# A graph network on one core: Elu and normalization by tile inside the projection of an attention layer, turned tiles copied by ScalarE, row terms stored beside the maximum

## The chip, the core and the metric

The kernel runs on one core of one Trainium2 chip. The metric is the device time of one execution in microseconds, from runs of the compiled program; the profile is of one execution more. All times below are microseconds (us) unless marked ns. PE is TensorE (matmul; PEld is its weight load), DVE VectorE, ACT ScalarE, POOL GpSimd, SP SyncE, which here only issues transfers.

## The reference

2500 nodes of 256 features and 40000 edges go through four parts: two graph attention layers of 8 heads of 32, a product with a masked matrix, three graph convolutions with a dense decoder, and one more attention of 4 heads of 64. Between the parts stand residual sums and a normalization with ReLU. The three attention layers are what the change touches.

```
def gat_conv(x, W, al, ar, b, src, dst):          # layers 1 and 2, H = 8, D = 32
    h = (x @ W).reshape(N, H, D)
    el = jnp.einsum('nhd,hd->nh', h, al)
    er = jnp.einsum('nhd,hd->nh', h, ar)
    e = jax.nn.leaky_relu(el[src] + er[dst], NEG_SLOPE)
    m = jax.ops.segment_max(e, dst, num_segments=N)
    ex = jnp.exp(e - m[dst])
    s = jax.ops.segment_sum(ex, dst, num_segments=N)
    alpha = ex / s[dst]
    out = jax.ops.segment_sum(alpha[:, :, None] * h[src], dst, num_segments=N)
    out = out.reshape(N, H * D) + b
    return jax.nn.elu(out)
...
x = gat_conv(features, W0, al0, ar0, b0, src, dst)
x = gat_conv(x, W1, al1, ar1, b1, src, dst)
```

Layer 1 reads relu(layernorm(x)); layer 2 reads the Elu of layer 1; the last attention (`_gat_head`, the same shape with 4 heads) reads relu(layernorm) of the decoder's output.

## The kernel before, in words

The 2500 nodes are 20 tiles (NT) of 128 rows. A matrix C of edge counts (16-bit, 20 x 2560 columns) stays in the core's memory, so that an attention is dense work on 128 x 1280 or 128 x 640 pieces of it. The program is a row of phases. Each phase has one instruction stream for each engine, and all engines meet at its end: the semaphores that the phase used are cleared, then comes a barrier (`Phase.__exit__`, which does so only where the phase owned a semaphore).

`attention(gat, nh, dh, split, norm, sgn, AB, scatter)` is called three times and has three phases:

1. The projection (lines 653 to 769). With `norm`, DVE takes mean and variance of all 20 tiles (L618, L624), ACT the root (L635), DVE the reciprocal and the shift (L627, L630). DVE multiplies the weights by the attention vectors and sums (the products, L696 and L700; they need the transfers of L679 and L681, or of L672 and L676 in the last attention). Then comes a loop over the tiles: ACT writes the tile `xn` (L738 with the normalization and ReLU, L741 a plain copy), PE turns it in two transposes (L753, "turn"), DVE copies it out of PSUM as `xT` (L710), PE multiplies by the weights (L760, "product", four instructions), and DVE takes the result: attention terms `AB` (L714), features `HB` (L715) and the largest magnitude `hmax` (L717). PSUM has two buffers of each kind. DVE's order in a step is xT of tile t, then the result of tile t-1. After the last tile PE turns the row terms (L769), DVE scales them (L726), SP stores them to DRAM (L685) and waits until they have landed.
2. The maximum and the exponentials (lines 787 to 930): a maximum over all nodes, four Exp by ACT, then ten rounds that write the factors UV and VP.
3. The heads (lines 945 to 1157): for each head and each part of C, SP loads one broadcast row of terms (`rows`, L991, two buffers), ACT compares (L1015), DVE masks (L1059, L1062), PE multiplies (L1146, L1154).

Between layer 1 and layer 2 stands a phase of its own, `elu` (L1165): five batches of four tiles, each with DVE bias sums (L1215), a minimum (L1220), ACT's Exp (L1256), a maximum (L1235) and a sum (L1241). Its result in HB is what L741 copies.

Of the kernel before, what the change touches and what calls it, by code (L numbers as in the profile page):

```python
# [15 lines left out]
P = 128  # L16
N = 2500
E = 40000
D = 256
# [48 lines left out]
def build(nc, x, src, dst, ew, gat0, gat1, sage, dec, gat3, out):  # L68
# [4 lines left out]
    with top:  # L73
# [567 lines left out]
        def attention(gat, nh, dh, split, norm, sgn, AB, scatter):  # L641
# [9 lines left out]
            HV = HB[:, :].rearrange("p (t c) -> p t c", t=NT)[:, :, 0:nh * (dh + 1)].rearrange("p t (h c) -> p t h c", c=dh + 1)  # L651

            with Phase() as ph:
# [3 lines left out]
                xn = ph.sb("xn", [P, 2, D], f32)  # L657
                xT = ph.sb("xT", [P, 2, D], f32)
                blocks = [(b, min(P, RT - b)) for b in range(0, RT, P)]
                rT = ph.sb("rT", [P, len(blocks) * P], f32)  # L660
                m_ = norm_memory(ph) if norm else None
                psT = [ph.ps(f"psT{u}", [P, D]) for u in range(2)]
                psH = [ph.ps(f"psH{u}", [P, W2]) for u in range(2)]
                psR = ph.ps("psR", [P, len(blocks) * P])
                s_tR, s_rT, s_w, s_wx, s_xn, s_T, s_xT, s_M, s_out, s_v, s_rd = (
                    ph.sem(n) for n in ("tR", "rT", "w", "wx", "xn", "T", "xT", "M", "out", "v", "rd"))
                block = ph.enter_context(nc.Block())
                @block.sync
                def _(sp):
                    if split:  # L670
# [12 lines left out]
                    sp.wait_ge(s_rT, len(blocks))  # L683
                    for n, (b, w) in enumerate(blocks):
                        sp.dma_start(rowd[b:b + w, :], rT[0:w, n * P:(n + 1) * P]).then_inc(s_rd, 16)  # L685
                    sp.wait_ge(s_rd, 16 * len(blocks))

                @block.vector
                def _(v):
                    ch = Chain(v, s_v)  # L690
                    if norm:
                        norm_vector(v, m_)
                    v.wait_ge(s_w, 16 * (3 * nh if split else 3))
                    for k in range(K):
                        for j in range(2):
                            ch(v.tensor_tensor(prod[:, 2 * k + j, :], Wx[:, k, 0:D], av[:, j, :], ALU.mult))  # L696
                    ch.wait()
                    for k in range(K):
                        for j in range(2):
                            last = v.tensor_reduce(Wx[:, k, D + j * nh:D + (j + 1) * nh],  # L700
                                                   prod[:, 2 * k + j, :].rearrange("p (h d) -> p h d", d=dh), AX.X,
                                                   ALU.add)
                    last.then_inc(s_wx, 1)
                    v.sem_inc(s_out, 6)
                    v.sem_inc(s_xT, 2)

                    def turned(t, u):
                        hold(v, s_T, t + 3)
                        hold(v, s_M, t + 1)
                        v.tensor_copy(xT[:, u, :], psT[u][:, :]).then_inc(s_xT, 1)  # L710

                    def result(t, u):
                        hold(v, s_M, t + 3)
                        v.tensor_copy(ABv[:, ds(t, 1), :], psH[u][:, D:W2].unsqueeze(1)).then_inc(s_out, 1)  # L714
                        v.tensor_copy(HV[:, ds(t, 1), :, 0:dh].rearrange("p t h c -> p (t h) c"),  # L715
                                      psH[u][:, 0:D].rearrange("p (h c) -> p h c", c=dh)).then_inc(s_out, 1)
                        v.tensor_reduce(hmax[:, ds(t, 1)], psH[u][:, 0:D], AX.X, ALU.max,  # L717
                                        apply_absolute_value=True).then_inc(s_out, 1)

                    def step(t, before, u):  # L720
                        turned(t, u)
                        result(before, 1 - u)
                    skewed(v, turned, step, result)
                    for n, (b, w) in enumerate(blocks):
                        v.wait_ge(s_tR, len(blocks))
                        v.tensor_scalar(rT[0:w, n * P:(n + 1) * P], psR[0:w, n * P:(n + 1) * P], BIG, None, ALU.mult  # L726
                                        ).then_inc(s_rT, 1)

                @block.scalar
                def _(a):  # L730
                    if norm:
                        norm_scalar(a, m_)
                    with a.Fori(0, NT // 2) as i:
                        for u in range(2):
                            t = i * 2 + u
                            hold(a, s_T, t + 1)
                            if norm:
                                a.activation(xn[:, u, :], XB[:, ds(t * D, D)], ACT.Relu, bias=m_["nmr"][:, ds(t, 1)],  # L738
                                             scale=m_["sd"][:, ds(t, 1)]).then_inc(s_xn, 1)
                            else:  # L740
                                a.activation(xn[:, u, :], HB[:, ds(t * TW, D)], ACT.Copy).then_inc(s_xn, 1)  # L741

                @block.tensor
                def _(pe):
                    pe.sem_inc(s_T, 2)
                    pe.sem_inc(s_M, 2)
                    pe.wait_ge(s_wx, 1)

                    def turn(t, u):
                        hold(pe, s_xn, t + 1)  # L750
                        hold(pe, s_xT, t + 1)
                        for k in range(K):
                            m = pe.transpose(psT[u][:, k * P:(k + 1) * P], xn[:, u, k * P:(k + 1) * P], ident[:, :])  # L753
                        m.then_inc(s_T, 1)

                    def product(t, u):
                        hold(pe, s_xT, t + 3)
                        hold(pe, s_out, t * 3 + 3)
                        for k in range(K):
                            m = pe.matmul(psH[u][:, :], xT[:, u, k * P:(k + 1) * P], Wx[:, k, :], start=k == 0, stop=k == K - 1)  # L760
                        m.then_inc(s_M, 1)

                    def step(t, before, u):
                        turn(t, u)
                        product(before, 1 - u)
                    skewed(pe, turn, step, product)
                    pe.wait_ge(s_out, 3 * NT + 6)
                    for n, (b, w) in enumerate(blocks):
                        pe.transpose(psR[0:w, n * P:(n + 1) * P], AB[:, RT + b:RT + b + w], ident[:, :]).then_inc(s_tR, 1)  # L769
# [6 lines left out]
            TH = NT * nh  # L776
            heads = Phase()
            with heads as hp:
                cB = hp.sb("cB", [P, TH], f32)
# [165 lines left out]
                with Phase() as ph:  # L945
# [39 lines left out]
                    def _(sp):  # L985
                        with sp.Fori(0, nh) as h:
                            for p in range(PARTS):
                                if TWO:
                                    hold(sp, s_Mn, (h * PARTS + p + 1) * len(TWO))
# [1005 lines left out]
```

## Time and profile before

| what | value |
|---|---|
| median of 3 runs | 2344.32 us (2344.3 to 2346.5) |
| the profiled execution's own time | 2345.53 us |
| its span | 2343.7 us |
| granted TensorE clock, mean | 0.909 |
| PE busy | 1751.7 us (75%) |
| DVE busy | 1668.3 us (71%) |
| ACT busy | 1378.9 us (59%) |
| POOL busy | 300.0 us (13%) |

The busy shares are means over phases with different limits. The change is read from the phases it touches: the first projection begins at 342.9 and its second phase at 393.0; the Elu phase begins at 779.9, the second projection at 804.4 and its second phase at 851.2; the last projection begins at 1936.5 and its second phase at 1985.7. The granted clock is a share of 2.4 GHz: 0.50 is 1.2 GHz, 1.00 is 2.4 GHz.

### The profile page before, as it was taken

The page shows a single profiled execution, that of the slowest core. Times are in us where ns is not written, and L with a number is a line of the kernel's source. Part 1 is how long each engine was busy: PE and PEld are TensorE (multiplying, and loading weights), DVE is VectorE, ACT ScalarE, POOL GpSimd, SP SyncE. Part 2 cuts the span into 40 slices and gives each one's busy share as a digit, 9 for nine tenths or more (in the row PEclk, how much of TensorE's full clock was granted, in tenths as well). Part 3 has the DMA queues.
Part 4 walks back from the last instruction along what each step waited for, and adds up shares of the span by engine and source line. Part 5 has one row for each costly group of instructions (what it writes and reads, how often), then busy time and mean ns, then how long its engine had stood idle before and what let it go on. Part 6 is the DMA issues. An engine that isn't in the chain of part 4 may idle for free. (4 is left out here: it accounts for less than half of the span.)

```text
span 2343.7 us, 65803 instructions
## 1 busy us (share of the span) xinstructions
PE 1751.7 (75%) x21987; PEld 1349.0 (58%) x21987; DVE 1668.3 (71%) x3799; ACT 1378.9 (59%) x2202; POOL 300.0 (13%) x460
## 2 busy tenths in 40 slices
PE   3998865599888336889981399994977995388881
PEld 1333323588888226888881256662546983388881
DVE  6988877899999678999997511113333246799997
ACT  0245763899999238999992411212122352699993
POOL 2465401556100020000000000000000000200000
PEclk9999987799999678999995699997998997699996
DMA  1000000111010001010001110000001010000002
GB/s 60 1 2 2 3 11 2 35 36 34 27 36 25 12 2 40 32 36 36 36 13 51 45 39 0 0 0 6 1 0 37 23 55 10 18 19 25 19 19 89
DMA packets 29718, 54.87 MB, mean 23 GB/s; under 512 B 10222, under 2 KB 20820, under 8 KB 29104
## 3 DMA queue, kind: packets, MB, share of 16 engines
q1 hardware_dynamic: 24608, 43.89, 5.5%
q0 software_dynamic: 4880, 7.80, 1.0%
q8 instruction: 158, 2.59, 0.4%
q14 instruction: 72, 0.59, 0.1%
HBM read 43.19 MB, written 8.49 MB: 22 GB/s over the span
## 5 line engine op out<-in xcount | busy, mean ns | idle before, releaser
L1146 PE MATMUL ps<-R,M 128*128 128x132 f16 (+1 forms) x8640 | 809.4, 221 | 217.4 <-DVE M L1059 112.2
L1015 ACT ACTIVATE Rm<-rows,cB 128x1280 bf16<-128x1280 f32 (+1 forms) x832 | 885.0, 1156 | 35.3 <-DMA rows<-rowd 16.1
L1146 PEld LDWEIGHTS ps<-R,M 128*128 128x128 f16 x8640 | 728.8, 97 | 260.7 <-issue 127.8
L1154 PE MATMUL ps<-HB,C 128*128 128x66 f16 x6400 | 597.0, 193 | 0.0
L1059 DVE TENSOR_TENSOR M<-Rm,C 128x1280 f16<-128x1280 bf16 (+1 forms) x832 | 555.4, 691 | 55.6 <-ACT Rm L1015 48.9
L1154 PEld LDWEIGHTS ps<-HB,C 128*128 128x128 f16 x6400 | 572.4, 97 | 0.0
L1419 PE MATMUL psA<-R,C 128*128 128x512 f16 (+1 forms) x1200 | 253.6, 350 | 96.5 <-POOL ones L1471 41.1
L546 DVE TENSOR_SCALAR ohc<-cells,near 128x1280 f16<-128x1280 f16 x387 | 214.0, 553 | 53.2 <-PE acc L571 47.4
L571 PE MATMUL acc<-ohc,ohl 128*128 128x420 f16 (+1 forms) x1161 | 244.5, 349 | 2.0 <-issue 0.4
L1419 PEld LDWEIGHTS psA<-R,C 128*128 (+1 forms) x1200 | 119.2, 99 | 193.7 <-issue 109.1
L1062 DVE SCALAR_TENSOR_TENSOR M<-rows,cN,C 128x1280 f16<-128x1280 f32 x128 | 197.9, 1546 | 0.0
L571 PEld LDWEIGHTS acc<-ohc,ohl 128*128 128x128 f16 x1161 | 90.2, 98 | 148.9 <-DVE ohl L548 86.7
L420 POOL DMA_INDIRECT wd<-wv,wi x104 | 122.7, 1180 | 135.1 <-issue 76.9
L530 ACT ACTIVATE C<-acc 128x420 f16<-128x420 f32 (+1 forms) x120 | 55.7, 543 | 125.6 <-PE acc L571 125.6
L1581 DVE TENSOR_SCALAR rdeg<-psD 128x1 f32 (+1 forms) x20 | 3.2, 158 | 171.6 <-ACT tl L1551 171.6
L548 DVE TENSOR_SCALAR ohl<-lows,bT 128x128 f16<-128x128 f16 x387 | 102.0, 264 | 0.0
L1049 DVE TENSOR_TENSOR Mn<-C,M 128x640 f16<-128x640 f16 x192 | 93.5, 487 | 0.6
L1149 PE MATMUL ps<-VS,C 128*128 128x130 f16 x640 | 88.3, 221 | 0.0
L1146 PE MATMUL ps<-R,Mn 128*128 128x130 f16 x960 | 86.8, 220 | 0.0
L760 PE MATMUL psH<-Wx,xT 128*128 128x272 f32 (+1 forms) x240 | 72.1, 426 | 16.0 <-DVE AB L714 14.3
L753 PE MATMUL psT<-ident,xn 128*128 128x128 f32 x120 | 24.9, 296 | 71.3 <-DVE Wx L700 71.3
L1510 PE MATMUL ps<-xT,W 128*128 128x128 f32 x640 | 76.3, 278 | 1.0 <-ACT xT L1555 1.0
(280 smaller groups left out, 2276.8 us busy)
## 6 DMA issues: line engine op xcount, KB each, us to landing
rows<-rowd SPq DMA_DIRECT2D x32, 640.0 KB, 3.8
rows<-rowd SPq DMA_DIRECT2D x16, 320.0 KB, 3.4
xd<-R SPq DMA_DIRECT2D x1, 2560.0 KB, 8.4
xr<-xd SPq DMA_DIRECT2D x20, 128.0 KB, 2.0
xd<-HB SPq DMA_DIRECT2D x1, 2560.0 KB, 9.9
xr<-xd POOLq DMA_DIRECT2D x1, 2560.0 KB, 9.3
R<-in_x SPq DMA_DIRECT2D x1, 2432.0 KB
R<-in_x POOLq DMA_DIRECT2D x1, 2432.0 KB
```

The costliest lines, as they stand in the source:

```text
L420: g.indirect_dma_start(out=wd[:, :], out_offset=bass.IndirectOffsetOnAxis(ap=m["wi"][w][:, :], axis=0), in_=m["wv"][w][:, :], in_offset=No ...
L546: v.tensor_scalar(ohc[:, u, :], cells[:, :], near[:, q % 2, ds(k, 1)], None, ALU.is_equal).then_inc(s_oh, 1)
L548: v.tensor_scalar(ohl[:, u, :], lows[:, :], bT[:, ds(k, 1)], None, ALU.is_equal).then_inc(s_oh, 1)
L571: ins = pe.matmul(bank(b, q % 2), ohl[:, u, :], ohc[:, u, d0 * NT:d1 * NT], start=first_, stop=True, skip_group_check=True)
L1015: a.activation(Rm[:, s % SG, :], rows[:, p % 2, :], ACT.Relu, bias=cB[:, ds(h + s * nh, 1)]).then_inc(s_R, 1)
L1049: v.tensor_tensor(Mn[:, u, :], Cs, M[:, u, :], ALU.subtract).then_inc(s_Mn, 1)
L1059: v.tensor_tensor(M[:, u, :], Rm[:, u, :], Cs, ALU.min).then_inc(s_M if s in ONE else s_cut, 1)
L1062: v.scalar_tensor_tensor(M[:, u, :], rows[:, p % 2, :], cN[:, ds(h + s * nh, 1)], Cs, ALU.is_gt, ALU.mult).then_inc(s_M, 1)
L1146: m = pe.matmul(region(p % 2, r), lhsT, rhs, start=first, stop=True, skip_group_check=True)
L1149: m = pe.matmul(region(p % 2, r), C[:, s * NP + p * W + (r % TP) * P:][:, 0:P], VS[:, TURNED.index(s), :, ds(h * cw, cw)], start=False, st ...
L1154: m = pe.matmul(both[:, :, cw:2 * cw], C[:, s * NP + p * W + r * P:][:, 0:P], VP[:, s, :, ds(h * cw, cw)], start=False, stop=True, skip_gr ...
L1419: m = pe.matmul(psA[:, :], lhsT, SPv[:, s, :, :].rearrange("p l c -> p (l c)"), start=s == 0, stop=s == NT - 1)
```

## The change

- The Elu phase between layers 1 and 2 is gone. Layer 2's projection loads the bias and does the Elu tile by tile: DVE adds the bias (`biased`), ACT writes relu(-z) and then exp of its negative (`negative`, `power`), DVE writes max(e - 1, z) (`unit`), and PE turns that.
- With normalization the statistics go in batches of five tiles (`stats`, `roots`, `scales`). The products come behind the first batch, the later batches stand between results.
- `xT` is copied by ACT (`turned`), no longer by DVE. The loops are written out.
- The turning and storing of the row terms is in the second phase, with ACT's copy in place of DVE's; the first two loads of `rows` are issued there too, and the third phase issues only the others. The two semaphores of `rows` now belong to the phase `heads` that encloses the second and third.

The core of the diff:

```diff
 @block.vector
+    def unit(t):
+        v.wait_ge(s_e, t + 1)
+        if t >= 4:
+            v.wait_ge(s_T, t - 3)
+        v.scalar_tensor_tensor(y[:, t % 4, :], e[:, t % 4, :], -1.0, z[:, t % 4, :], ALU.add,
+                               ALU.max).then_inc(s_y, 1)
...
     if norm:
-        norm_vector(v, m_)
...
+        stats(0)
+        products()
+        stats(1)
+        scales(0)
+        for b in range(NT // FIVE):
+            if b + 2 < NT // FIVE:
+                stats(b + 2)
+            if b + 1 < NT // FIVE:
+                scales(b + 1)
+            for t in batch(b):
+                result(t)
+    else:
+        for i in range(NT + 4):
+            if i < NT:
+                biased(i)
+            if i == 3:
+                products()
+            if 0 <= i - 2 < NT:
+                unit(i - 2)
+            if i >= 4:
+                result(i - 4)
 @block.scalar
+    def turned(t):
+        a.wait_ge(s_T, t + 1)
+        if t >= 2:
+            a.wait_ge(s_M, t - 1)
+        a.activation(xT[:, t % 2, :], psT[t % 2][:, :], ACT.Copy).then_inc(s_xT, 1)
+    if norm:
+        roots(0)
+        for i in range(NT + 1):
+            if i < NT:
+                normal(i)
+                if i % FIVE == 2 and i // FIVE + 1 < NT // FIVE:
+                    roots(i // FIVE + 1)
+            if i:
+                turned(i - 1)
+    else:
+        for i in range(NT + 3):
+            if i < NT:
+                negative(i)
+            if 0 <= i - 1 < NT:
+                power(i - 1)
+            if i >= 3:
+                turned(i - 3)
 @block.tensor
+    def turn(t):
+        pe.wait_ge(s_y, t + 1)
+        if t >= 2:
+            pe.wait_ge(s_xT, t - 1)
...
+    def product(t):
+        pe.wait_ge(s_xT, t + 1)
+        if t == 0:
+            pe.wait_ge(s_wx, 2 * K)
+        if t >= 2:
+            pe.wait_ge(s_out, (t - 1) * 3)
...
+    for i in range(NT + 1):
+        if i < NT:
+            turn(i)
+        if i:
+            product(i - 1)
 # second phase
+    @block.sync
+    def _(sp):
+        for n, (b, w) in enumerate(blocks):
+            sp.wait_ge(s_rT, n + 1)
+            sp.dma_start(rowd[b:b + w, :], rT[0:w, n * P:(n + 1) * P]).then_inc(s_rd, 16)
+        sp.wait_ge(s_rd, 16 * len(blocks))
+        for q in range(2):
+            sp.dma_start(rows[:, q, :], row_terms[q, 0:1, :].to_broadcast([P, W])).then_inc(s_row[q], 16)
...
-attention(gat0[0:3], 8, 32, False, True, 1, AB, True)
-elu(R[:, :], HB, gat0[3], 8, False, pitch=TW)
-attention(gat1[0:3], 8, 32, False, False, 1, AB, False)
+attention(gat0[0:3], 8, 32, False, None, 1, AB, True)
+attention(gat1[0:3], 8, 32, False, gat0[3], 1, AB, False)
```

How it moves DVE's work at the head of the first projection (st and mv are the statistics, sd and nmr the scale and the shift, prod and Wx the products). Before:

```order
L618 BN_STATS st<-R 128x6 x20
L624 BN_AGGR mv<-st 128x2 x20
L627 RECIPROCAL sd<-sd 128x20
L630 SCALAR_TENSOR_TENSOR nmr<-mv,sd 128x20
L696 TENSOR_TENSOR prod<-Wx,av 128x256 x4
L700 TENSOR_REDUCE Wx<-prod 128x8 x4
L710 COPY xT<-psT_83 128x256
```

DVE at the same place now:

```order
L710 BN_STATS st<-R 128x6 x5
L713 BN_AGGR mv<-st 128x2 x5
L700 TENSOR_TENSOR prod<-Wx,av 128x256 x4
L704 TENSOR_REDUCE Wx<-prod 128x8 x4
L710 BN_STATS st<-R 128x6 x5
L713 BN_AGGR mv<-st 128x2 x5
L718 RECIPROCAL sd<-sd 128x5
L721 SCALAR_TENSOR_TENSOR nmr<-mv,sd 128x5
L710 BN_STATS st<-R 128x6 x5
L713 BN_AGGR mv<-st 128x2 x5
L718 RECIPROCAL sd<-sd 128x5
L721 SCALAR_TENSOR_TENSOR nmr<-mv,sd 128x5
```

The products moved ahead of the first scales, and only then come the first reciprocal and shift that release ACT's first tile.

DVE at the head of the second projection (AB and HB are the result's terms and features), before:

```order
L696 TENSOR_TENSOR prod<-Wx,av 128x256 x4
L700 TENSOR_REDUCE Wx<-prod 128x8 x4
L710 COPY xT<-psT_179 128x256
L597 UNCONDITIONAL_BRANCH
L597 ISA
L149 REGISTER_ALU
L710 COPY xT<-psT_180 128x256
L149 REGISTER_ALU
L714 ISA
L714 COPY AB<-psH_181 128x16
L715 ISA
L715 COPY HB<-psH_181 128x8x32
```

DVE at the same place now, where z is the sum with the bias, e ACT's exponential and y the Elu's result:

```order
L727 TENSOR_TENSOR z<-R,bias 128x256 x3
L734 SCALAR_TENSOR_TENSOR y<-e,z 128x256
L727 TENSOR_TENSOR z<-R,bias 128x256
L696 TENSOR_TENSOR prod<-Wx,av 128x256 x4
L704 TENSOR_REDUCE Wx<-prod 128x8 x4
L734 SCALAR_TENSOR_TENSOR y<-e,z 128x256
L727 TENSOR_TENSOR z<-R,bias 128x256
L734 SCALAR_TENSOR_TENSOR y<-e,z 128x256
L740 COPY AB<-psH_178 128x16
L741 COPY HB<-psH_178 128x8x32
L742 TENSOR_REDUCE hmax<-psH_178 128x1
```

The copy of xT left DVE; in a step stand now z of tile i, y of tile i-2 and the result of tile i-4, and the products come behind the fourth z.

SP around the second layer's row terms, before:

```order
L679 DMA Wx<-in_L_gnn_W 128x2x256
L681 DMA av<-in_L_gnn_al 128x256
L681 DMA av<-in_L_gnn_ar 128x256
L685 DMA rowd<-rT 128x128
L685 DMA rowd<-rT 32x128
L98 UNCONDITIONAL_BRANCH
L984 UNCONDITIONAL_BRANCH
L986 UNCONDITIONAL_BRANCH
L986 ISA
L991 ISA
L991 DMA rows<-rowd 128x1280
```

SP at the same place now:

```order
L678 DMA bias<-in_L_gnn_b 128x256
L688 DMA Wx<-in_L_gnn_W 128x2x256
L690 DMA av<-in_L_gnn_al 128x256
L690 DMA av<-in_L_gnn_ar 128x256
L98 UNCONDITIONAL_BRANCH
L911 UNCONDITIONAL_BRANCH
L915 DMA rowd<-rT 128x128
L915 DMA rowd<-rT 32x128
L918 DMA rows<-rowd 128x1280 x2
L98 UNCONDITIONAL_BRANCH
L1078 UNCONDITIONAL_BRANCH
L1085 DMA rows<-rowd 128x1280 x14
```

The stores and the first two loads moved past the end of the projection (its L98), the loads past the end of the second phase as well; the bias comes ahead of the weights.

## Rows read from the trace of the kernel before

**Rows 1.** Windows: stretch, length, busy of PE, PEld, DVE, ACT, POOL, clock, DMA, GB/s.
```profile
358.60:389.20 30.60, 25.09 (x114) 18.26 (x112) 23.16 (x78) 9.62 (x16) 0.00 (x0) 0.97 0.00 0
816.00:847.30 31.30, 25.26 (x114) 18.30 (x112) 23.24 (x78) 6.68 (x16) 0.00 (x0) 0.98 0.00 0
```

**Rows 2.** Timeline, first projection's head: start, duration, engine, line, [idle before <-releaser].
```profile
342.90 6.63 DVE L618 BATCH_NORM_STATS2 st<-R 128x6 f32<-128x256 f32 x20 [7.34 <-PEq L101]
...
349.57 1.43 DVE L624 BATCH_NORM_AGGREGATE mv<-st 128x2 f32<-128x6 f32 x20
...
352.29 1.09 ACT L738 ACTIVATE xn<-R,nmr,sd 128x256 f32 x2 [0.94 <-DVE nmr L630]
...
356.68 2.15 PE L760 MATMUL psH<-Wx,xT 128*128 128x272 f32 x4 [0.58 <-DVE xT L710]
...
359.06 0.19 DVE L714 COPY AB<-psH 128x16 f32 x1 [2.21 <-PE psH L760]
```

**Rows 3.** Timeline, PE in the first projection's loop: turn, product, next turn.
```profile
363.55 0.38 PE L753 MATMUL psT<-ident,xn 128*128 128x128 f32 x2
...
363.83 1.16 PE L760 MATMUL psH<-Wx,xT 128*128 128x272 f32 x4
...
364.82 0.38 PE L753 MATMUL psT<-ident,xn 128*128 128x128 f32 x2
```

**Rows 4.** Timeline, the first projection's last tile, its row terms, the next phase.
```profile
386.29 0.41 DVE L710 COPY xT<-psT 128x256 f32<-128x256 f32 x1
...
386.97 0.76 PEld L760 LDWEIGHTS psH<-Wx,xT 128*128 128x128 f32 x4 [1.01 <-issue]
387.00 1.16 PE L760 MATMUL psH<-Wx,xT 128*128 128x272 f32 x4 [0.61 <-DVE AB L714]
...
388.30 0.19 DVE L714 COPY AB<-psH 128x16 f32<-128x16 f32 x1 [0.86 <-PE psH L760]
...
388.73 0.41 DVE L717 TENSOR_REDUCE hmax<-psH 128x1 f32<-128x256 f32 x1
...
390.18 0.82 SPq L685 DMA_DIRECT2D rowd<-rT  x2
392.97 0.20 POOL L818 MEMSET one<- 9x128 f32 x1 [56.19 <-POOLq L101]
```

**Rows 5.** Timeline, the Elu phase and the second projection's first instructions.
```profile
783.03 1.10 DVE L1215 TENSOR_TENSOR HB<-R,bias 128x256 f32<-128x256 f32 x3 [4.05 <-DMA bias<-in_L_gnn_b]
...
791.42 1.06 ACT L1256 ACTIVATE e<-e 128x1024 f32<-128x1024 f32 x1 [3.08 <-DVE e L1220]
...
802.28 1.23 DVE L1241 TENSOR_TENSOR HB<-HB,e 128x1024 f32<-128x1024 f32 x1
804.36 0.39 SPq L679 DMA_DIRECT2D Wx<-in_L_gnn_W  x1
804.70 0.72 ACT L741 ACTIVATE xn<-HB 128x256 f32 x2 [3.97 <-PEq L745]
```

**Rows 6.** DMA issues of the Elu phase and second projection: count, size, us to landing.
```profile
bias<-in_L_gnn_b SPq DMA_DIRECT2D x1, 128.0 KB, 3.1
...
av<-in_L_gnn_ar SPq DMA_DIRECT2D x1, 128.0 KB, 4.2
```

**Rows 7.** Timeline, first DVE instruction of the second layer's second phase.
```profile
851.28 0.57 DVE L836 TENSOR_SCALAR XC<-AB 128x160 f32<-128x160 f32 x1 [2.99 <-PEq L101]
```

**Rows 8.** Timeline, the last weight transfers of the last projection.
```profile
1941.28 0.94 SPq L676 DMA_DIRECT2D av<-in_L_gnn_a  x2
```

**Rows 9.** DMA issues of the last projection.
```profile
av<-in_L_gnn_a SPq DMA_DIRECT2D x8, 32.0 KB, 2.7
```

**Rows 10.** Line L1555, ACT's copies out of PSUM in a later phase: ns min/median/max.
```profile
L1555 ACT ACTIVATE xT<-psT x20: 597/597/597, 1360.3 to 1595.7; 128x512 f32<-128x512 f32 x20
```

**Rows 11.** Timeline, the first loads of rows in the heads and ACT's first comparison.
```profile
429.63 0.99 SPq L991 DMA_DIRECT2D rows<-rowd  x2
...
433.81 3.87 ACT L1015 ACTIVATE Rm<-rows,cB 128x1280 bf16<-128x1280 f32 x3 [5.41 <-DMA rows<-rowd]
```

More of the change, by code:

```diff
@@ L693, in _ @@
[L693 to L727, printed above, removed]
+                    def products():
+                        v.wait_ge(s_w, 16 * (3 * nh if split else 3))
+                        for k in range(K):
+                            for j in range(2):
+                                v.tensor_tensor(prod[:, 2 * k + j, :], Wx[:, k, 0:D], av[:, j, :], ALU.mult).then_inc(s_pr, 1)
+                        v.wait_ge(s_pr, 2 * K)
+                        for k in range(K):
+                            for j in range(2):
+                                v.tensor_reduce(Wx[:, k, D + j * nh:D + (j + 1) * nh],
+                                                prod[:, 2 * k + j, :].rearrange("p (h d) -> p h d", d=dh), AX.X,
+                                                ALU.add).then_inc(s_wx, 1)
@@ L729, in _, with roots @@
                 @block.scalar
                 def _(a):
-                    if norm:
[L732 to L741, printed above, removed]
+                    def roots(b):
+                        some = slice(b * FIVE, (b + 1) * FIVE)
+                        a.wait_ge(s_mv, (b + 1) * FIVE)
+                        var = mv[:, :].rearrange("p (t c) -> p t c", c=2)[:, some, 1]
+                        a.activation(sd[:, some], var, ACT.Sqrt, bias=eps[:, 0:1]).then_inc(s_sd, 1)
@@ L776, in attention @@
             TH = NT * nh
+            PARTS = 4 if split else 2
+            TP = NT // PARTS
+            W = TP * P
+            row_terms = rowd[0:RT, :].rearrange("(h p t) j -> p h (t j)", h=nh, p=PARTS)
             heads = Phase()
             with heads as hp:
+                rows = hp.sb("rows", [P, 2, W], f32)
+                s_row = [hp.sem(f"row{b}") for b in range(2)]
                 cB = hp.sb("cB", [P, TH], f32)
@@ L957, in attention @@
                     ps = [[ph.ps(f"ps{b}{j}", [P, 3 * 2 * XW]) for j in range(NB)] for b in range(2)]
-                    s_row = [ph.sem(f"row{b}") for b in range(2)]
                     s_R, s_M, s_Mn, s_cut, s_P, s_E, s_tl, s_v = (
```

125 lines of the change are left out of this document (79 added, 46 removed).

## The prediction

> **What bounds the kernel now.** I read the stages by windows first, then the timeline at the head, in the loop and at the tail of each projection, then the transfers' landing times. In the two windowed loops neither PE nor DVE is full: PE works 25.09 of 30.60 us and DVE 23.16, and the second layer's loop reads alike [rows 1]. A tile costs about 1.5 us (30.6 over 20). The reader should see why: PE alone could go from turn to turn in 364.82 - 363.55 = 1.27 us [rows 3], but DVE has four instructions in a tile, and the xT copy stands in its queue between the results that PE waits for. Around the loops lie stretches in which hardly anything runs: the head until the first result at 359.06 [rows 2], the row terms' store between the last result and 392.97 [rows 4], the whole Elu phase, where DVE works and PE stands [rows 5], and 4.2 us at the head of each heads phase, where everything waits for the first row [rows 11]. None of it lies beside other work that bounds the end, since all engines meet at each phase's end. So every microsecond here counts in full.
>
> **Part 1, the Elu phase and the second projection.** Before, they last from 779.9 (the bias lands after 3.1 us and the first sum starts at 783.03 [rows 5, 6]) to 851.28 [rows 7]. I build the new stage up from the same start.
> Head: DVE starts its first z at 783.0. The attention vectors are issued last, behind the bias: 0.4 us later than the 0.95 us that they now have behind the first weight issue, so at 781.25, and land 4.2 us later [rows 6], at 785.5. By then DVE has done four z and one y. Products: eight instructions of 0.36 us, 2.9 us, to 788.4. Then y of tile 1, its turn, and product 0, which at the low clock takes 2.15 us [rows 2]: first result at 792.0, first step done at 792.7.
> Loop: the order of the queues closes a ring over two steps. Step i on DVE is z(i), y(i-2), result(i-4). ACT copies xT(i-3) behind relu and exp of its own step, and those begin when z(i) is there. From the start of z: 0.45 until ACT's first, two issues of 0.31 (ACT's pair takes 0.72 with 0.42 for one [rows 5]), then the copy 0.40, so xT at 1.46. From xT's end (386.70) to the weights' load (386.97) is 0.27, from there to AB (388.30) 1.33, from AB to the last reduction's issue (388.73) 0.43, and 0.34 more until DVE can issue again [rows 4]. Together 3.83 us, and then the z of two steps later may start: 1.92 us a tile. DVE's own work is only 0.34 x 4 + 0.1 = 1.45, PE's 1.27. Step 5 starts at 792.7, and step 19, seven rings later, at 819.5; the last four products no longer wait for z and go at 1.3, which brings the last reduction's end to 827.7. A phase's end costs 0.85 us (803.51 to 804.36 [rows 5]). So the second phase starts at 828.6 instead of 851.28: **-22.7**.
> Prices the trace doesn't show: ACT's copy of 128x256 float out of PSUM. It is at most the 0.60 of 128x512 and at least half of that, 0.30 [rows 10]; I take 0.40. Exp of 256 is between 0.40 and the 1.06 of 1024 [rows 5]; I take 0.40, since the difference to the plain copy's 0.42 is all length. y as a two-operand DVE instruction: 0.42, like L1215 (three in 1.10 [rows 5]). If both ACT prices were at their upper ends, the ring would be 4.7 and the stage 8 us longer; if the ring didn't bind, 1.45 a tile, 9 us shorter.
> [...]
>
> **Part 2, the first projection.** Before: 342.90 to 392.97. DVE's statistics of five tiles take 6.63/4 + 1.43/4 = 2.0 [rows 2], to 345.0; the products, which were covered by 20 tiles of statistics, now wait for the vectors. By [rows 6], 4.2 after an issue 0.95 behind the first, they land at 348.0. Products to 350.95, second statistics to 353.1, scales to 353.5. ACT's first tile then starts at 353.5, 1.2 later than the 352.29 of before [rows 2]. But PE no longer waits for two tiles ahead: turn, copy, turn, product 0 at low clock give the first result at 358.0 instead of 359.06. The third statistics and scales (2.4) fit before it. Then 19 tiles at PE's 1.27 (24.1), 1 us of low clock, 1.1 for the statistics that now stand between results 4 and 5 (PE has two PSUM buffers, 2.5 us of DVE are more than these hold), 0.8 of last result: 385.1. End of phase 0.9: 386.0, that is **-7.0**; of this 2.9 is the store and its landing, which no longer stand at the end [rows 4].
> Bounds: at the old 1.5 us a tile the gain would be 2.5; without the 1.1 and the low clock it would be 9.
>
> **Part 3, the last projection.** Twelve transfers instead of three. The last starts at about 1941.8 and lands 2.7 later [rows 8, 9], at 1944.5. Before, DVE had statistics until then. Now it stands still from 1938.6: products to 1947.4, statistics and scales to 1950.0, the first result 4.5 later at 1954.5, some 1.9 later than before. The loop and its end as in part 2 (27.0) give 1981.5, the next phase 1982.4 instead of 1985.7: **-3.3**, between 0 and -7.
>
> **Part 4, the row terms in the second phase.** PE's transposes, ACT's copies, SP's stores and the loads lie beside 36 us of DVE work. Nothing waits for them there: ACT's table load moves behind its copies but is through before DVE needs Exp. When heads begins, rows are there, so ACT's first comparison starts 0.1 after the phase and not at 433.81: 4.1 us [rows 11], three times, **-12.2**. The same mask, product and transfer order follows, so nothing else is late next: DVE waits 1.4 for that comparison before and after.
> Against it: heads now owns two semaphores, so its end has a clearing and a barrier of its own. A whole phase's end is 0.85; the extra part is between 0 and that. I take 0.4, three times, **+1.2**.
>
> **Sum.** -22.7 - 7.0 - 3.3 - 12.2 + 1.2 = -44.0. The profiled execution took 2345.53, its span 2343.7; so it would take 2301.5. The median of the runs is 1.2 lower, which gives 2300.3. I say 2301.
>
> **Rivals.**
> (a) The ring doesn't close; the Elu stage goes at DVE's 1.45 a tile: 9 us less, 2292. For it: ACT may copy an earlier xT while DVE is late. Against: the order of its queue is fixed, and xT(i-3) stands behind relu(i). 0.15.
> (b) The normalized projections bring nothing: the products wait for weights, the statistics in the loop stop PE twice, and the pace stays at 1.5. Then parts 2 and 3 are only the store, 2.9 + 2.2, and the total is 39 less: 2306. For it: DVE has 2.4 + 5 x 0.77 = 6.3 us of work in a batch, exactly PE's 5 x 1.27. 0.22.
> (c) The early loads of rows do not do what they say, because something else (the comparison's code, the first mask) is as late as the row was: 12 us back, 2313. Against: ACT is named as waiting for this transfer for 5.41 [rows 11]. 0.07.
> (d) Slower: PE's clock stays at 1.2 GHz through the three loops. In the Elu stage PE has 1.27 of work in 1.92 us, less dense than the 25.09 of 30.60 that now hold 0.97 of full clock [rows 1]. A product at the low level takes 2.15 against 1.16 [rows 2, 3], so a tile 2.35 instead of 1.27: 38 tiles x 1.08 = 41, and the Elu ring 0.5 a tile more, 9: 2351. It decides from seven eighths of the tiles at the low level. 0.03.
> The Trainium skill (TensorE: Matmul & The Clock Gate, A second HAM failure mode: psum-queue depth-cycling) tells of such a clock that swings where PE idles briefly between groups while it cycles through PSUM buffers; by that rule (d) would be likelier. The present loops idle briefly in every tile and cycle through two buffers, and hold 0.97 and 0.98, so the trace speaks against it here.
>
> **Numbers.** The forecast has 0.5, its own range 2296 to 2306; 0.03 is left for what I don't see. With (a), (b) and part of (c), and the unknown prices of part 1 (8 us up, 9 down), the range is 2290 to 2313. Only (d) and a sum of all bad ends reach the old time: faster by more than 0.2% 0.96, within 0.2% (what a measurement can tell from no change) 0.01, slower 0.03.
>
> **What would show it.** Second projection: z at 1.9 us from step to step, DVE waiting for the product in each; 1.45 would be (a). First result of the last projection later than before, of the first a little earlier. In both normalized loops, AB 1.27 apart, with one gap behind the fifth tile. ACT's first comparison within 0.3 us of the heads' start. The clock at 0.95 or more in the loops. I am wrong if the Elu stage isn't under 52 us, or if a new wait on ACT stands in a loop.

## The result, and the profile after

The changed kernel takes 2287.78 us (median of 4 runs, 2287.27 to 2289.7) against 2345.41 (4 runs, 2344.3 to 2346.53) on the same chip: ratio 0.9756, 95% interval 0.9739 to 0.9773. The profiled span falls from 2343.7 to 2287.9. The direction was as forecast, and so were the mechanisms but for the pace of the loops. The gain was larger: 55.8 us in the spans and 57.6 in the medians, where 44 was worked out, and the time lies 2.2 us under the forecast range.

Landmarks that both traces have show where it went (first statistics or last copy of the heads, first `XC` of the second phase, first `Rm` of the heads):

| stretch | before | after | difference | forecast |
|---|---|---|---|---|
| first projection, statistics to `XC` | 50.11 | 40.34 | -9.8 | -7.0 |
| `XC` to first `Rm`, layers 1, 2, 3 | 40.80, 40.74, 42.66 | 36.38, 36.50, 39.38 | -11.9 | -12.2 |
| end of heads 1 to second `XC` (Elu and projection) | 72.63 | 46.55 | -26.1 | -22.7 |
| last projection, statistics to `XC` | 49.27 | 42.27 | -7.0 | -3.3 |
| all the rest | | | -1.0 | +1.2 |

The forecast's +1.2 stands for the heads' own ends; one of the three lies within the third stretch.

The windows over the three loops, for [rows 1] (columns as there):

```profile
356.50:382.00 25.50, 22.70 (x113) 17.93 (x111) 19.15 (x74) 15.19 (x36) 0.00 (x0) 0.97 0.00 1
777.00:809.00 32.00, 27.43 (x113) 16.83 (x111) 27.19 (x92) 16.26 (x49) 0.00 (x0) 0.98 0.00 1
1903.00:1932.00 29.00, 24.57 (x120) 19.38 (x120) 22.27 (x94) 18.10 (x43) 0.00 (x0) 0.92 0.00 1
```

In the first window PE works 22.70 of 25.50 us (89%), before 25.09 of 30.60 for the same tiles. The granted clock is 0.97, 0.98 and 0.92 (the last window begins with 4.8 us at 1.2 GHz; from the first result on, it is 1.00), so rival (d) is out. The Trainium skill's rule on depth-cycling (TensorE: Matmul & The Clock Gate, A second HAM failure mode: psum-queue depth-cycling), by which it would have been likelier, is not borne out by these rows. The timeline of the normalized loop, for [rows 3], up to the fifth tile:

```profile
359.56 0.38 PE L827 MATMUL psT<-ident,y 128*128 128x128 f32 x2
...
359.78 1.08 PE L837 MATMUL psH<-Wx,xT 128*128 128x272 f32 x4
...
359.98 0.38 ACT L799 ACTIVATE xT<-psT 128x256 f32<-128x256 f32 x1 [0.27 <-PE psT L827]
...
360.70 0.38 PE L827 MATMUL psT<-ident,y 128*128 128x128 f32 x2
...
362.79 1.72 DVE L710 BATCH_NORM_STATS2 st<-R 128x6 f32<-128x256 f32 x5
...
363.19 1.08 PE L837 MATMUL psH<-Wx,xT 128*128 128x272 f32 x4
...
365.18 0.18 DVE L740 COPY AB<-psH 128x16 f32<-128x16 f32 x1
...
366.15 0.70 PE L837 MATMUL psH<-Wx,xT 128*128 128x272 f32 x2 [1.66 <-DVE AB L740]
```

From turn to turn it is 1.14 us where 1.27 was forecast; ACT's copy takes 0.38 and runs beside PE's work. The gap behind the fifth tile is real: PE idles 1.66 us for DVE. The second projection, one step in the middle:

```profile
779.49 0.42 DVE L727 TENSOR_TENSOR z<-R,bias 128x256 f32<-128x256 f32 x1
...
779.94 0.42 ACT L789 ACTIVATE e<-z 128x256 f32<-128x256 f32 x1 [0.69 <-DVE z L727]
780.26 0.40 ACT L793 ACTIVATE e<-e 128x256 f32<-128x256 f32 x1
...
780.57 0.36 ACT L799 ACTIVATE xT<-psT 128x256 f32<-128x256 f32 x1
...
780.99 1.18 PE L837 MATMUL psH<-Wx,xT 128*128 128x272 f32 x4 [0.25 <-ACT xT L799]
...
782.21 0.19 DVE L740 COPY AB<-psH 128x16 f32<-128x16 f32 x1 [0.18 <-PE psH L837]
...
782.63 0.41 DVE L742 TENSOR_REDUCE hmax<-psH 128x1 f32<-128x256 f32 x1
...
782.96 0.42 DVE L727 TENSOR_TENSOR z<-R,bias 128x256 f32<-128x256 f32 x1
```

This is the ring of the prediction, station for station: z, relu, exp, copy, product, result, and z of two steps later. It takes 3.47 us (782.96 - 779.49), not 3.83. DVE at the head of the last projection:

```profile
1890.44 1.73 DVE L710 BATCH_NORM_STATS2 st<-R 128x6 f32<-128x256 f32 x5 [1.19 <-PEq L101]
...
1898.66 1.43 DVE L700 TENSOR_TENSOR prod<-Wx,av 128x256 f32<-128x256 f32 x4 [6.01 <-DMA av<-in_L_gnn_a]
...
1907.94 0.17 DVE L740 COPY AB<-psH 128x8 f32<-128x8 f32 x1 [1.12 <-PE psH L837]
```

DVE stands 6.01 us for the twelve transfers. The first result comes 17.5 after the first statistics, 1.4 later than before (forecast 1.9 later). And where the row was waited for [rows 11], ACT's first comparison:

```profile
418.93 1.36 ACT L1109 ACTIVATE Rm<-rows,cB 128x1280 bf16<-128x1280 f32 x1 [1.11 <-DVEq L1132]
```

It comes with the phase's own start and no longer waits for a transfer, so rival (c) is out too.

### The profile page after: what moved, and what is told of

It reads as the page before. It is cut to its first block and busy times, and to the rows that moved or that the text cites. A ratio compares the mean times of both kernels' runs of the same rounds, so it can differ in the third digit from the quotient of the medians.

```text
span 2287.9 us, 64776 instructions
## 1 busy us (share of the span) xinstructions
PE 1750.4 (77%) x21987; PEld 1348.8 (59%) x21987; DVE 1639.7 (72%) x3751; ACT 1398.4 (61%) x2288; POOL 302.1 (13%) x460
## 5 line engine op out<-in xcount | busy, mean ns | idle before, releaser
L1153 DVE TENSOR_TENSOR M<-Rm,C 128x1280 f16<-128x1280 bf16 (+1 forms) x832 | 556.2, 693 | 42.6 <-ACT Rm L1109 34.0
L1652 ACT ACTIVATE hT<-ps,b0c 128x128 f32<-128x128 f32 x80 | 22.9, 368 | 87.0 <-PE ps L1603 87.0
```

Source lines behind the costliest of these rows:

```text
L1153: v.tensor_tensor(M[:, u, :], Rm[:, u, :], Cs, ALU.min).then_inc(s_M if s in ONE else s_cut, 1)
```

## The experiments

All kernels of this section assert bounds on some values that engines load from the table of edge chunks. That lengthens the stage ahead of the first projection by 12 us. So the changed kernel was run in this form too (`x0_bounded`), and the others stand against it or, where they start from the kernel before, against one another and by the lengths of their phases. A time of these kernels holds the 12 us, while the 2345 us of the kernel before don't.

**The changed kernel with bounds.**

```diff
-return eng.value_load(table[0:1, q:q + 1])
+return eng.value_load(table[0:1, q:q + 1], min_val=2 * PACK, max_val=(NCH + 1) * PACK)
```

> The changed kernel, with bounds asserted on the values that the stage ahead of the first projection loads from its table. Every experiment below has these bounds, so this is what they are compared with. Both theories: nothing moves from the first projection on; the stage ahead of it is 0 to 3 us longer, for some 160 more small register instructions; 2288 to 2291.

Measured: 2303.13 (2301.29 to 2304.22), span 2300.6. The expectation missed: the bounds cost 12 to 15 us. They stand ahead of the first projection, which starts at 354.26 instead of 342.21; it is 40.07 long (40.34 without bounds). One later phase is not alike: the last projection takes 43.70, against 42.27 without bounds and 42.2 to 42.6 in e1, e5 and e8, whose edits don't touch it. Its first results fall in a stretch in which TensorE still has 1.2 GHz, and come 2.19 and 1.49 apart instead of 1.1:

```profile
1919.74:1922.50 2.76, 2.76 (x9) 2.19 (x8) 1.40 (x6) 1.01 (x3) 0.00 (x0) 0.50 0.00 0
```

In the changed kernel without bounds the clock is at 2.4 GHz from the first result on. So 1.1 to 1.4 us of every difference to this profile's last projection are the clock and not the edit.

**The loops.** The pace was forecast from the old loops, where every wait has a second instruction (`hold`: a wait and an addition to an unused semaphore) and the tile number is a register. Three kernels take this apart. The changed kernel with `hold` on PE:

```diff
-pe.wait_ge(s_xT, t + 1)
+hold(pe, s_xT, t + 1)        # and PE's other waits in turn and product
```

> The changed kernel with each of PE's waits in the projection (turn and product) followed by a semaphore increment, as in the kernel before (hold). Theory: the increments stand in PE's queue between a wait and the matmul, and the 1.27 us from turn to turn and the 0.27 from xT to the weights that the prediction took from the trace of before contain them. Then the normalized loops go from 1.14 back to about 1.27 a tile, the Elu stage from 1.74 to about 1.87 a step, and the time rises by 6 to 9 us. Rival: ACT's copy signals PE sooner than DVE's did, and the increments cost nothing: pace 1.14 and 1.74 as now, time within 1 us.

Measured: 2301.59 (2300.34 to 2304.3), span 2298.5. The expectation missed: the time overlaps with x0's. The normalized loops didn't change (1.14 a tile, first projection 40.1), as the rival had it. Only the ring became slower, as the theory had it: from first to last z 34.9 us instead of 33.3, and two steps take 3.68 instead of 3.47. In the total this doesn't show, in part because the last projection is 1.1 shorter than x0's.

The kernel before with its projection loops written out, the waits plain:

```diff
-with a.Fori(0, NT // 2) as i:
+for i in range(NT // 2):     # skewed() of DVE and PE written out as well
...
-hold(v, s_T, t + 3)
+v.wait_ge(s_T, t + 3)        # every hold of the projection
```

> The kernel before, with the projection's three loops written out and plain waits in place of hold; DVE still copies xT, nothing else of the change is in it. Theory (queue overhead): the loop's registers and increments made up most of the 1.5 us a tile, so the pace falls to 1.15 to 1.25 and the time by 12 to 18 us to 2327 to 2333. Rival (the prediction's reason: the xT copy stands in DVE's queue between the results that PE waits for): the pace stays at 1.4 to 1.5, the time falls by under 5 us.

Measured: 2337.49 (2334.28 to 2340.8). The expectation was set without the 12 us of the bounds; with them the fall is some 20 us, more than either theory had, while the pace of 1.24 a tile in the first projection is the first theory's. That projection is 43.5 long instead of 50.1 although DVE still copies xT. And the same with the loops written out but `hold` kept:

> The kernel before with only one thing changed: the projection's loops are written out, the waits keep their second instruction (a semaphore add behind each wait), and the waits' values are constants because the tile number is. Compare with the same kernel with plain waits (2337.5 us, span 2337.4; its first projection 43.4 us). Theory: the loop's registers are the cost, the second instruction hardly any: 2337 to 2341, first projection 43.4 to 44.5, pace 1.22 to 1.27. Rival: the second instruction of each wait is half of it: first projection 46 to 47, total 2347 or more.

Measured: 2348.66 (2346.41 to 2351.43), first projection 48.4; without the 12 us it would lie under the kernel before. The rival's main point holds: the second instruction is over half of it (the first projection is longer than even the rival had). From first to last result the three projections take 29.24, 29.64 and 29.17 in the kernel before, 27.75, 27.24 and 26.69 with written-out loops, and 23.55, 24.24 and 23.78 with plain waits as well. These sums hold a few tiles at 1.2 GHz at the start, not the same number in each; in the even stretches two results of the first projection take 3.00, 2.77 and 2.44 us. PE and its releaser in the kernel with `hold`:

```profile
380.22 0.38 PE L763 MATMUL psT<-ident,xn 128*128 128x128 f32 x2
...
381.28 0.41 DVE L720 COPY xT<-psT 128x256 f32<-128x256 f32 x1
381.36 0.38 PE L763 MATMUL psT<-ident,xn 128*128 128x128 f32 x2
...
381.96 0.76 PEld L770 LDWEIGHTS psH<-Wx,xT 128*128 128x128 f32 x4 [0.46 <-issue]
...
382.98 0.38 PE L763 MATMUL psT<-ident,xn 128*128 128x128 f32 x2
...
383.30 0.18 DVE L724 COPY AB<-psH 128x16 f32<-128x16 f32 x1 [0.46 <-PE psH L770]
```

And with plain waits:

```profile
380.02 0.41 DVE L720 COPY xT<-psT 128x256 f32<-128x256 f32 x1
380.20 0.38 PE L763 MATMUL psT<-ident,xn 128*128 128x128 f32 x2
...
380.48 0.76 PEld L770 LDWEIGHTS psH<-Wx,xT 128*128 128x128 f32 x4
...
381.51 0.38 PE L763 MATMUL psT<-ident,xn 128*128 128x128 f32 x2
...
381.71 0.19 DVE L724 COPY AB<-psH 128x16 f32<-128x16 f32 x1
```

And in the kernel before: the wait inside [rows 3], then turns without a wait, then a tile with one:

```profile
363.03 0.41 DVE L710 COPY xT<-psT 128x256 f32<-128x256 f32 x1
...
363.80 0.30 PEld L760 LDWEIGHTS psH<-Wx,xT 128*128 128x128 f32 x2
...
369.85 0.38 PE L753 MATMUL psT<-ident,xn 128*128 128x128 f32 x2
...
370.99 0.38 PE L753 MATMUL psT<-ident,xn 128*128 128x128 f32 x2
...
371.05 0.41 DVE L710 COPY xT<-psT 128x256 f32<-128x256 f32 x1
...
371.83 0.76 PEld L760 LDWEIGHTS psH<-Wx,xT 128*128 128x128 f32 x4 [0.70 <-issue]
...
373.25 0.19 DVE L714 COPY AB<-psH 128x16 f32 x1 [0.65 <-PE psH L760]
```

Three things are read here. Where PE doesn't wait, the turns are 1.14 apart in every form: with `hold` (380.22 to 381.36) and in the hardware loop of the kernel before too (369.85 to 370.99). So 1.14 was PE's own pace all along. The 1.27 of [rows 3] was a pair in which PE waited for xT: the copy ended at 363.44, and the weights' load came 0.36 later, as in every tile with a wait.

Where PE does wait, xT's end to the weights' load is 0.36 in the hardware loop (363.44 to 363.80), 0.27 written out with `hold` (381.69 to 381.96) and 0.05 with plain waits (380.43 to 380.48). The tile of [rows 4], with its 0.27, is the last one and stands behind the loop. From the weights' load to `AB`, where DVE waits, it is 1.42, 1.34 and 1.23 (371.83, 381.96 and 380.48 to the next lines with `AB`). So register work takes some 0.09 in each of the two handovers. PE passes two `hold`s behind xT, for 0.22, and DVE one in front of `AB`, for 0.11: each addition costs 0.11. The ring with `hold` on PE alone agrees: 0.27 and 1.22 (790.46, 790.73, 791.95 in e1).

The turn behind such a wait then comes 1.62 after the last one instead of 1.31.

**xT back on DVE**, in the changed kernel:

```diff
                                 power(i - 1)          # ACT
-                            if i >= 3:
-                                turned(i - 3)
...
                                 unit(i - 2)           # DVE
+                            if 0 <= i - 3 < NT:
+                                turned(i - 3)         # and by tile in the normalized loops
```

> The changed kernel with one part undone: DVE copies xT again, in all three projections; the loops stay written out. Compare with the bounded changed kernel (2303.1 us, span 2300.6). Theory: the copy in DVE's queue was worth little; the pace came from the hardware loop. The normalized loops go from 1.14 to 1.22 us a tile (20 tiles, +1.6 each), the Elu projection becomes bound by DVE at about 1.9 us a step (+3 to +5). Total +6 to +9, so 2309 to 2312. Rival, the reason the prediction gave (the copy stands between the results that PE waits for): the normalized loops return to 1.5 us a tile, +7 each, and the Elu stage +5: 2322 or more.

Measured: 2311.26 (2309.87 to 2316.66), +8.1 as the theory had it, but not where it had it. In the profiled execution, the slowest of the four, the first projection is 6.8 longer, the second 1.2, the last 5.0. Where only results stand, the copy costs what was expected (1.22 a tile). What I had left out is DVE's queue at a batch of statistics:

```profile
377.55 0.19 DVE L740 COPY AB<-psH 128x16 f32<-128x16 f32 x1
...
378.30 1.72 DVE L710 BATCH_NORM_STATS2 st<-R 128x6 f32<-128x256 f32 x5
...
381.02 0.18 DVE L740 COPY AB<-psH 128x16 f32<-128x16 f32 x1
...
381.16 1.92 PE L845 MATMUL psH<-Wx,xT 128*128 128x272 f32 x4 [2.30 <-DVE xT L749]
...
383.12 0.19 DVE L740 COPY AB<-psH 128x16 f32<-128x16 f32 x1 [0.94 <-PE psH L845]
...
385.20 0.19 DVE L740 COPY AB<-psH 128x16 f32<-128x16 f32 x1 [0.92 <-PE psH L845]
```

The window between them (columns as in [rows 1]):

```profile
381.50:384.90 3.40, 3.40 (x10) 2.58 (x9) 1.84 (x7) 1.18 (x3) 0.00 (x0) 0.50 0.00 0
```

Behind the statistics there is a gap of 3.5 from the result at 377.55, in which PE stands 2.30 us for a copy queued behind them. With the copy on ACT, PE goes on with its next turn and copy meanwhile, and stands 1.66. The next two tiles take 2.1 each, but not by a wait: PE is busy in all 3.40 us of the window, at a clock of 0.50. The clock fell to 1.2 GHz right behind the stand of 2.30 us, and it did so once more in the last projection (a stand of 2.32 us, then 0.50 from 1941.4 to 1944.8). Behind the stands of 1.66 and 1.70 in the changed kernel it didn't. So of the 6.8 us in the first projection some 1.7 are these two tiles (2.09 each instead of 1.22), and some 1.5 are the first two tiles of the loop, more of which lie at the low clock than in x0. The other three executions took 5 to 7 us less than this one; whether their clock fell in mid-loop too isn't on record.

**The ring.** ACT's order in the second projection:

```diff
 for i in range(NT + 3):
+    if i >= 3:
+        turned(i - 3)
     if i < NT:
         negative(i)
     if 0 <= i - 1 < NT:
         power(i - 1)
-    if i >= 3:
-        turned(i - 3)
```

> The changed kernel with ACT's order in the Elu projection altered: the xT copy of tile i-3 stands ahead of the relu of tile i, not behind relu and exp. Compare with the bounded changed kernel (2303.1, span 2300.6; from the first z 33.2 us to the last). Theory (the ring through z, relu, exp, copy, product, result): it opens, and the step falls from 1.74 us to DVE's own work of about 1.45: -4 to -6, so 2297 to 2299. Rival (DVE's own queue is the bound already, the ring only looks closed): no change, 2303.

Measured: 2299.33 (2297.35 to 2300.74), -3.8, just short of what was expected; from first z to `XC` it is 37.5 us instead of 41.3. From first to last z it is 29.9 us instead of 33.3, 1.57 a step on average. In the middle DVE goes through its queue almost without a stand, at steps of 1.42 and 1.53 in turn:

```profile
795.29 0.41 DVE L727 TENSOR_TENSOR z<-R,bias 128x256 f32<-128x256 f32 x1
...
796.71 0.42 DVE L727 TENSOR_TENSOR z<-R,bias 128x256 f32<-128x256 f32 x1
```

This pair is 1.42 apart. The ring was closed, and one order of two lines opens it.

**The statistics.** First in the last projection alone, with three batches and the first scales ahead of the products:

```diff
+scales(0); stats(1); stats(2)
 products()
-stats(1)
-scales(0)
```

> The changed kernel with DVE's order at the head of the last projection altered: statistics of three batches and the first scales stand ahead of the products, which wait for the eight late vectors. Compare with the bounded changed kernel (2303.1, span 2300.6). Theory: the 6.0 us in which DVE stood for the vectors is filled with 4 us of statistics that no longer stand between later results and at the head: -4 to -5, 2298 to 2299. Rival: the vectors bound the first result anyway and the statistics moved were hidden in the loop: -1 or less.

Measured: 2298.36 (2297.25 to 2299.26), -4.8. DVE's wait for the vectors shrinks from 6 us to what is left behind the statistics, and the first result comes 13.35 after the first statistics instead of 17.48. The phase is 39.91 long, 3.8 less than x0's and 2.4 less than without bounds. The loop gives some of the earlier start back, since its first two results now come at 1.2 GHz, 2.19 and 1.84 apart. DVE's wait:

```profile
1910.26 1.43 DVE L700 TENSOR_TENSOR prod<-Wx,av 128x256 f32<-128x256 f32 x4 [1.03 <-DMA av<-in_L_gnn_a]
```

Then all four batches ahead, in both normalized projections:

```diff
-stats(0); products(); stats(1); scales(0)
+for b in range(NT // FIVE):
+    stats(b)
+scales(0); products()
```

> The changed kernel with the statistics of all 20 tiles ahead of the first scales and the products, in both normalized projections (ACT's roots stay by fives). Compare with the bounded changed kernel (2303.1, span 2300.6; first projection 14.6 us to the first result and 23.8 from first to last, last projection 17.5 and 24.4). Theory: what counts is only whether DVE's statistics stand beside a wait for the vectors. First projection: 8 us of statistics against about 5 us until the vectors land, so the first result is 3 to 4 us later, but the gap in the loop (about 2) and the second one go: +1 to +2. Last projection: the first result 3.5 to 4.5 earlier and no gap: -5 to -6. Total -3 to -5: 2298 to 2300. Rival (spreading the statistics is what made the loops short): first projection +5, last 0, total 2308.

Measured: 2294.05 (2290.69 to 2295.41), -9.1, twice what I expected. The last projection is 38.64 long, 5.1 less than x0's 43.70 but 3.6 less than the 42.27 without bounds, which is the fairer figure: the first result comes 3.65 earlier and the gap is gone, and two tiles at the low clock (2.19 and 2.02 apart) cost 2.0 of it. The first, for which I expected a loss, gains 2.6 (37.51 instead of 40.07): its first result comes 13.87 after the first statistics, not 3 to 4 later but 0.8 earlier, for the vectors had been waited for 2.9 us and the second and third batch had already stood ahead of the first result, and the loop loses its gap (21.98 from first to last result instead of 23.78).

**The heads' own end.**

```diff
-s_row = [hp.sem(f"row{b}") for b in range(2)]
+s_row = [nc.alloc_semaphore(f"row{b}_{names[0]}") for b in range(2)]   # cleared with the third phase
```

> The changed kernel with the two semaphores of rows cleared at the third phase's end, so that heads owns none and has no clearing and barrier of its own. Compare with the bounded changed kernel (2303.1, span 2300.6). Theory (the prediction's 0.4 us for each of three such ends): -1.2, 2301.9. Rival: the cost is that of a whole phase's end, 0.85 each: -2.6, or nothing that the trace shows: 2303.

Measured: 2300.23 (2297.17 to 2301.75). The runs overlap with those of x0; the trace is sharper: from the heads' last copy to the next phase's first transfer 1.26 us (775.68 to 776.94) against 1.78 (774.70 to 776.48). 0.52 for each of three, -1.6 in all, if the other two are alike.

**Together.** The edits of the ring, of the three batches in the last projection and of the heads' end in one kernel:

> Three edits together: the xT copy ahead of relu in the Elu projection, the statistics of three batches ahead of the products in the last projection, and one barrier less at the end of each heads. Alone the first gave -3.8 and the second -4.8 against the bounded changed kernel (2303.1), the third is expected at -1.2. They lie in different phases, so they should add: -9.8, 2293.3. Rival: they share a cause (the clock or the transfers) and add to less than 8.

Measured: 2292.58 (2291.07 to 2293.03), -10.6: they add (3.8, 4.8 and 1.6). With the three edits and the statistics fitted to each wait:

```diff
+early = 4 if split else 2      # split: the last projection
+stats(0); scales(0)
+for b in range(1, early):
+    stats(b)
+products()
```

> The three edits together, and the statistics fitted to each wait: in the first projection the second batch and the first scales stand ahead of the products too, in the last all four batches do. Theory (DVE's statistics are free as long as the vectors have not landed): against the three together the first projection loses its wait of about 3 us less the 2 already needed for scales: -1.5 to -2.5, the last one another -1 to -2: about 2290. Rival: the first result of the last projection is bound by the vectors and the gap in the loop was hidden: 2293, as the three together.

Measured: 2287.24 (2286.53 to 2289.59), -15.9 against the changed kernel with the same bounds; against the kernel before the ratio is 0.9752 (0.9739 to 0.9765), with the 12 us of the bounds in it. It was not measured without them. That is 5.3 less than the three together, where 2.5 to 4.5 was expected. The phase lengths are 37.54 and 38.93 in the first and last projection (40.07 and 43.70) and, from first z to `XC`, 38.55 in the second (41.32). In the first projection DVE now waits only 0.21 for the vectors:

```profile
358.99 1.43 DVE L700 TENSOR_TENSOR prod<-Wx,av 128x256 f32<-128x256 f32 x4 [0.21 <-DMA av<-in_L_gnn_ar]
```

## Why the prediction came out short, point by point

- **What bounds the kernel:** the stretches around the loops counted in full, as said: removed, they came back nearly one for one in the total. What I said of the loop itself was half right. I put the pace of 1.5 us down to the xT copy in DVE's queue. The experiments show that most of it was the loop's form: 1.54 a tile, 1.43 written out, 1.25 with plain waits, with the copy still on DVE. The copy's own share is 0.1 a tile in an even stretch (1.22 against 1.14). With statistics between the results it is more, +6.8 and +5.0 a projection in the profiled execution with xT back on DVE, but nearly half of the first figure is the low clock in that execution.
- **What the record adds to this:** written-out loops with plain waits took 6.6 off the first projection and 6.3 off the last (e2), the moved row terms 2.5 and 2.4 (e4). If the two add, which no run shows, then the batches of statistics and ACT's copies together gave 0.7 in the first and cost 1.7 in the last. It was the later placements of the statistics (e6, e7, e11) that made them pay.
- **The step that failed** is in the durations: "PE's 1.27" and the handovers of the ring, 0.27 from xT's end to the weights' load and 1.33 from there to `AB`. I took them from [rows 3, 4] as properties of the operations. The 1.27 was a pair of turns in which PE waited for xT; PE's own is 1.14, which the same trace shows at 369.85. The 0.27 held two additions (0.22) and the 1.33 one (0.11), which the change removes, because it writes the loops with plain waits. I priced them at nothing.
- **Part 1, -22.7 against -26.1.** The ring exists and binds (e5). Of its stations the handover was 0.06 for 0.27, weights to `AB` 1.22 for 1.33, the copy 0.36 for 0.40; 0.36 less in all, 2.5 us over seven rings; 0.33 of the 0.36 are the three additions. The first result came 8.0 after the first z, not 9.0, and the end from the last z to `XC` took 8.1, not 9.1. Against these, the bias landed 3.6 after its issue, not 3.1, and the heads' own end, 0.5, lies in this stretch. Rival (a), a ring that doesn't close, is out.
- **Part 2, -7.0 against -9.8.** 19 tiles at 1.14 instead of 1.27 are 2.5. The first result came at 14.5 (forecast 15.1 after the first statistics). The gap for the statistics cost 1.8 (363.19 to 366.15, less 1.14) where I had 1.1, and the low clock at the start 0.8 where I had 1. Rival (b) had this gap's cause right (6.3 us of DVE work in a batch), but PE stood once for it, not twice, and its 1.5 us a tile is refuted.
- **Part 3, -3.3 against -7.0.** The wait for the twelve transfers was placed and sized well (until 8.2 after the start, forecast 8.0). The first result is 1.4 later than before, forecast 1.9; the rest, some 3 us, is the loop: 22.97 from first to last result where 24.1 and a gap were allowed. The gap is as in part 2 (1.9 in both, from the results' distances), but the loop starts at 2.4 GHz, and its turns are 1.11 apart (a product has 264 columns here, not 272).
- **Part 4, -12.2 and +1.2, against -11.9 and +1.6.** The +1.6 is three times the 0.52 of e8. The rest is shown by the kernel before with this part alone:

```diff
-sp.wait_ge(s_rd, 16 * len(blocks))       # with the stores, at the projection's end
+for q in range(2):                       # second phase, behind the stores there
+    sp.dma_start(rows[:, q, :], row_terms[q, 0:1, :].to_broadcast([P, W])).then_inc(s_row[q], 16)
```

> The kernel before, with only the row terms moved: turned, scaled and stored in the second phase, and the first two loads of rows issued there. Theory: 4.1 us at the head of each heads phase and the store and its landing at each projection's end (2.9, 2.9, 2.2) go, two more barriers of some 0.4 each come with them: 18 to 20 us less than before, 2325 to 2327. Rival: something else is as late as the row, so only the 8 us of the stores go: 2336.

Measured: 2336.86 (2335.78 to 2337.97), with the 12 us of the bounds, which the expectation didn't have; the number alone would have fitted the rival. By its phases: 4.4, 4.2 and 3.7 off from `XC` to `Rm`, and 2.5, 2.9 and 2.4 off the projections, whose ends no longer hold the store: 20.1 in all, as the theory had it.
- **The price of ACT's copy** was taken as 0.40 without a row for this shape. A copy of 128x256 out of PSUM takes ACT 0.36 to 0.38, beside DVE's 0.41, so moving it to ACT doesn't lengthen the ring. The step between two z is 1.74 on average, forecast 1.92.
- **The range.** Its lower end allowed for cheaper ACT instructions in part 1 but kept the 1.27 and the handovers as fixed in all three parts. One error in a shared term moves all parts the same way, which a sum of separate bounds doesn't show.

## What to carry to other kernels

A gap between two instructions belongs to the form of the code around them: register work and a second instruction behind a wait are in it. Before taking it over to code written in another way, look at what issues the instruction. And before calling a distance an engine's own pace, read it at several places of the loop: the shortest one, in which nothing was waited for, is the floor. Where an engine must wait for a transfer, put work there that stands in a loop otherwise. Where a queue closes a ring through three engines, look for the one instruction whose input is ready earliest and move it to the front.

## What the runs showed of the hardware that was not expected

- An addition to a semaphore behind a wait costs 0.11 us each time the engine really waits: two of them 0.22 on PE (0.27 against 0.05 from release to weight load), one 0.11 on DVE (1.34 against 1.23 from weight load to the result's copy). It costs nothing where PE comes late anyway (1.14 a tile with and without).
- The register work of a hardware loop's waits costs 0.09 us more in each such handover here (0.36 against 0.27 and 1.42 against 1.34), and nothing where PE doesn't wait (1.14).
- TensorE's clock fell to 1.2 GHz for 3.4 us in the middle of a loop behind one stand of PE of 2.30 and 2.32 us (e3, the two normalized projections), and stayed at 2.4 GHz behind stands of 1.66 and 1.70 us. An earlier first result also met the low clock for longer: with the result 3.65 us earlier, two tiles at the low clock took 2.0 us back (e7).
- Asserted bounds on loaded values cost 12 us in one stage, in which they stand between the loads and the work that they steer.
- Statistics in a loop of two PSUM buffers cost more where a PSUM copy stands in the same queue: PE stood 2.30 us for them instead of 1.66.
